# Attention's mix of a graph network: one fp32 product replaced by two rounded-fp32 products of high and low parts

## The reference

```
msg = xl[src] + xr[dst];  act = where(msg > 0, msg, 0.2 * msg)
e = sum(act * att, head)
p = exp(e - max of the node)
out[node] = sum over its edges of p * xl[src] / (sum of p + 1e-16)
```

## Time and profile before

| | us |
|---|---|
| median of 3 runs | 1897.4 |
| the profiled execution, its own time | 1914.85 |
| its span | 1913.0 |
| attention's steady part, about 468 to 889 in the span | 421 |

### The profile page before, as it was taken

One profiled execution on the slowest core, in us unless ns is written; L12 is line 12 of the kernel. 1 busy time (PEld: TensorE's weight loads), 2 busy tenths in 40 slices (PEclk: granted clock), 3 DMA queues, 4 the chain that ended last, 5 costly groups with the idle time before them and its releaser, 6 DMA issues.

```text
span 1913.0 us, 21680 instructions
## 1 busy us (share of the span) xinstructions
PE 1629.2 (85%) x8385; PEld 1359.4 (71%) x8385; DVE 844.1 (44%) x1268; ACT 454.1 (24%) x788; POOL 274.7 (14%) x265
## 2 busy tenths in 40 slices
PE   0887993745999999995549998699999989999996
PEld 0886883735777777784438887588888868878885
DVE  6785554542666755664552223432311142332233
ACT  3773111422222322221330101311201031121000
POOL 3000000015455443530220000000000000000000
PEclk9996997976878877887769999799999999999998
DMA  0345334143333332322552221422422242243221
GB/s 10 94 113 200 132 121 166 49 112 100 94 104 106 111 99 83 99 68 101 170 183 73 86 72 69 156 92 85 161 84 72 105 154 88 102 138 118 106 94 66
DMA packets 100475, 202.58 MB, mean 106 GB/s; under 512 B 24774, under 2 KB 58846, under 8 KB 100378
## 3 DMA queue, kind: packets, MB, share of 16 engines
q1 hardware_dynamic: 84474, 152.65, 23.8%
q0 software_dynamic: 15904, 48.61, 8.3%
HBM read 147.29 MB, written 53.92 MB: 105 GB/s over the span
## 4 chain that ended last, share of the span: by engine, by line
PE 42%; DMA 4%; DVE 3%; ACT 2%; DVEq 2%; issue 1%; POOL 0%; SPq 0%; POOLq 0%; ACTq 0%
PE layers_y_ps L1591 27%; PE layers_sum_ps L1555 13%; PE layers_turn_ps L1574 2%; DMA layers_raw<-in_L_gnn_W_self 1%; DMA layers_raw<-in_L_gnn_W_neigh 1%; DVE layers_w_lo L1701 1%; ACT layers_w_hi L1638 1%; DVEq L1739 1%; DMA layers_raw<-in_L_gnn_W 1%; DVE layers_y L710 1%; ACT layers_plain L1671 0%; DVEq L1745 0%; DVE layers_ln_stats L704 0%; DVEq L705 0%; DMA layers_x<-hidden_d 0%
## 5 line engine op out<-in xcount | busy, mean ns | idle before, releaser
L1138 POOL DMA_INDIRECT attention_got<-xl_d,attention_src x200 | 213.8, 1069 | 585.0 <-DMA attention_src<-in_src_held 380.7
L1744 DVE TENSOR_TENSOR layers_y<-layers_y_ps,layers_side 128x1024 f32<-128x1024 f32 x50 | 61.2, 1224 | 492.9 <-PE layers_y_ps L1591 488.6
L1591 PE MATMUL layers_y_ps<-layers_w_hi,layers_turned_hi 128*128 128x512 f32 x840 | 270.4, 404 | 9.6 <-DVE layers_turned_lo L1709 9.6
L1591 PE MATMUL layers_y_ps<-layers_w_lo,layers_turned_hi 128*128 128x512 f32 x840 | 265.6, 398 | 0.0
L1591 PE MATMUL layers_y_ps<-layers_w_hi,layers_turned_lo 128*128 128x512 f32 x840 | 263.8, 396 | 0.0
L1555 PE MATMUL layers_sum_ps<-layers_parts_hi,layers_counts 128*128 128x512 f32 x600 | 189.0, 396 | 8.7 <-POOL layers_parts_lo L1532 8.7
L1591 PEld LDWEIGHTS layers_y_ps<-layers_w_hi,layers_turned_hi 128*128 128x128 f32 x840 | 160.4, 195 | 42.7 <-DVE layers_turned_lo L1709 11.3
L1591 PEld LDWEIGHTS layers_y_ps<-layers_w_lo,layers_turned_hi 128*128 128x128 f32 x840 | 162.5, 193 | 35.1
L1555 PE MATMUL layers_sum_ps<-layers_parts_lo,layers_counts 128*128 128x512 f32 x600 | 186.3, 392 | 0.0
L1591 PEld LDWEIGHTS layers_y_ps<-layers_w_hi,layers_turned_lo 128*128 128x128 f32 x840 | 161.5, 192 | 34.9
L1555 PEld LDWEIGHTS layers_sum_ps<-layers_parts_hi,layers_counts 128*128 128x128 f32 x600 | 111.7, 190 | 31.0 <-issue 9.1
(11 more groups left out here) (247 smaller groups left out, 2231.7 us busy)
## 6 DMA issues: line engine op xcount, KB each, us to landing
layers_x<-x_d SPq DMA_DIRECT2D x40, 512.0 KB, 3.4
layers_counts<-counts_d SPq DMA_DIRECT2D x30, 640.0 KB, 3.9
attention_dst_wide<-in_dst_held SPq DMA_DIRECT2D x20, 640.0 KB
x_d<-layers_y SPq DMA_DIRECT2D x20, 512.0 KB, 2.7
self_d<-layers_y SPq DMA_DIRECT2D x20, 512.0 KB, 2.9
layers_side<-self_d SPq DMA_DIRECT2D x20, 512.0 KB, 4.2
layers_raw<-in_L_gnn_W_self POOLq DMA_DIRECT2D x16, 512.0 KB, 4.5
layers_raw<-in_L_gnn_W_neigh POOLq DMA_DIRECT2D x16, 512.0 KB, 4.3
```

What stands on the lines that cost most here:

```text
L1138: pool.indirect_dma_start(got[s][:, t, :], None, xl_d, bass.IndirectOffsetOnAxis(src[s][:, t:t + 1], 0))\
L1591: last = nc.tensor.matmul(y_ps[n % 2][:, a:a + HALF], rows_in[:, k, :], w[:, begin + k, a:a + HALF], start=(k == 0 and p == 0), stop=(k == ...
L1744: nc.vector.tensor_tensor(out, product, side[:, :], ALU.add).then_inc(y_ps_free, 1)
```

## The change

`hot` becomes a rounded-fp32 tile (F32R). The weighted rows are split: ScalarE rounds them to `mix_hi` (`take_high`), VectorE subtracts that from them and rounds the rest to `mix_lo` (`take_low`), each in two halves of 5 tiles x 260 columns. `mix` multiplies `hot` by all high tiles of the half, then by all low tiles: again 10 products per half, but rounded-fp32 ones with one record each. `take_high` of half 0 stands at the end of ScalarE's step q = 4, that of half 1 at the end of the next q = 0; `take_low` of half 0 in VectorE's q = 0 (after `find_nodes`), that of half 1 in q = 1 (after `take_best`). Both halves of `mix` come two steps later than before: half 0 in q = 1 instead of the q = 4 before it, half 1 in q = 2 instead of q = 0. `finish` moves from q = 1 to q = 2. Each loop that takes part runs one step longer.

```diff
--- before.py
+++ after.py
@@ -1059,8 +1059,10 @@
         shift = slots("shift", [P, KH, 2], F32R)
         clamped = slots("clamped", [P, SUB_TILES, HEADS])
         keep = slots("keep", [SUB, HEADS])
-        hot = slots("hot", [P, SUB_TILES, SUB])
+        hot = slots("hot", [P, SUB_TILES, SUB], F32R)
         weighted = slots("weighted", [P, SUB_TILES, HEADS, HEAD_DIM + 1])
+        mix_hi = slots("mix_hi", [P, SUB_TILES, HEADS * (HEAD_DIM + 1)], F32R)
+        mix_lo = slots("mix_lo", [P, SUB_TILES, HEADS * (HEAD_DIM + 1)], F32R)
         inverse = m.sb("inverse", [SUB, HEADS])
         mixed = slots("mixed", [SUB, HID])
         nothing = m.sb("nothing", [ROWS - SUB * SUBS, HID])
@@ -1078,7 +1080,11 @@
             m.sem(n) for n in "hot_t_ready message_ready scaled_ready bent_ready bent_r_ready scored maxed".split())
         shift_ready, shifted, clamp_ready, exp_ready, keep_ready, hot_ready = (
             m.sem(n) for n in "shift_ready shifted clamp_ready exp_ready keep_ready hot_ready".split())
-        weighed, mixed_in, out_ready = (m.sem(n) for n in "weighed mixed_in out_ready".split())
+        weighed, mix_hi_ready, mix_lo_ready, mixed_in, out_ready = (
+            m.sem(n) for n in "weighed mix_hi_ready mix_lo_ready mixed_in out_ready".split())
+
+        def half_of(tiles, half):
+            return tiles[:, half * PAIRS_HELD:(half + 1) * PAIRS_HELD]
         mixed_stored = m.sems("mixed_stored")
         block = m.block(gpsimd_works=True)
 
@@ -1202,17 +1208,19 @@
 
             def mix(j, half):
                 tiles = range(half * PAIRS_HELD, (half + 1) * PAIRS_HELD)
-                pe.wait_ge(weighed, 2 * j + half + 1)
+                pe.wait_ge(mix_lo_ready, 2 * j + half + 1)
                 if half == 0 and j >= 2:
                     pe.wait_ge(out_ready, j - 1)
-                for t in tiles:
-                    last = nc.tensor.matmul(mix_ps[j % 2][:, :, :].rearrange("p h d -> p (h d)"), hot[j % 2][:, t, :],
-                                            weighted[j % 2][:, t].rearrange("p h d -> p (h d)"), start=(t == 0),
-                                            stop=(t == SUB_TILES - 1))
+                for part in (mix_hi, mix_lo):
+                    for t in tiles:
+                        last = nc.tensor.matmul(mix_ps[j % 2][:, :, :].rearrange("p h d -> p (h d)"),
+                                                hot[j % 2][:, t, :], part[j % 2][:, t, :],
+                                                start=(t == 0 and part is mix_hi),
+                                                stop=(t == SUB_TILES - 1 and part is mix_lo))
                 if half:
                     last.then_inc(mixed_in, 1)
 
-            for i in range(LAST + PAIRS_HELD + 2):
+            for i in range(LAST + PAIRS_HELD + 3):
                 j, q = i // PAIRS_HELD, i % PAIRS_HELD
                 if i < LAST:
                     messages(i)
@@ -1220,9 +1228,9 @@
                     take_shift(j - 1)
                 if 2 <= i < LAST + 2:
                     score(i - 2)
-                if q == 4 and 1 <= j <= SUBS:
-                    mix(j - 1, 0)
-                if q == 0 and j >= 2:
+                if q == 1 and j >= 2:
+                    mix(j - 2, 0)
+                if q == 2 and j >= 2:
                     mix(j - 2, 1)
 
         @block.scalar
@@ -1258,7 +1266,13 @@
                 nc.scalar.activation(weighted[b][:, :, :, HEAD_DIM], clamped[b][:, :, :], ACT.Exp)\
                     .then_inc(exp_ready, 1)
 
-            for i in range(LAST + PAIRS_HELD):
+            def take_high(j, half):
+                act.wait_ge(weighed, 2 * j + half + 1)
+                nc.scalar.activation(half_of(mix_hi[j % 2], half).rearrange("p t c -> p (t c)"),
+                                     half_of(weighted[j % 2], half).rearrange("p t h d -> p (t h d)"), ACT.Copy)\
+                    .then_inc(mix_hi_ready, 1)
+
+            for i in range(LAST + PAIRS_HELD + 1):
                 j, q = i // PAIRS_HELD, i % PAIRS_HELD
                 if i < LAST:
                     scale(i)
@@ -1266,6 +1280,10 @@
                     exponentials(j - 1)
                 if i < LAST:
                     bend(i)
+                if q == 4 and j >= 1:
+                    take_high(j - 1, 0)
+                if q == 0 and j >= 2:
+                    take_high(j - 2, 1)
 
         @block.vector
         def _(dve):
@@ -1362,8 +1380,15 @@
                                         inverse[:, :].unsqueeze(2).to_broadcast([SUB, HEADS, HEAD_DIM]), ALU.mult)\
                     .then_inc(out_ready, 1)
 
+            def take_low(j, half):
+                dve.wait_ge(mix_hi_ready, 2 * j + half + 1)
+                nc.vector.tensor_tensor(half_of(mix_lo[j % 2], half).rearrange("p t c -> p (t c)"),
+                                        half_of(weighted[j % 2], half).rearrange("p t h d -> p (t h d)"),
+                                        half_of(mix_hi[j % 2], half).rearrange("p t c -> p (t c)").bitcast(F32),
+                                        ALU.subtract).then_inc(mix_lo_ready, 1)
+
             find_nodes(0)
-            for i in range(LAST + PAIRS_HELD + 2):
+            for i in range(LAST + PAIRS_HELD + 3):
                 j, q = i // PAIRS_HELD, i % PAIRS_HELD
                 if i < LAST:
                     bend(i)
@@ -1381,7 +1406,11 @@
                     weigh(j - 1, 0)
                 if q == 4 and 1 <= j <= SUBS:
                     weigh(j - 1, 1)
+                if q == 0 and j >= 2:
+                    take_low(j - 2, 0)
                 if q == 1 and j >= 2:
+                    take_low(j - 2, 1)
+                if q == 2 and j >= 2:
                     finish(j - 2)
 
 
```

## The result

| | us |
|---|---|
| after, median of 6 runs (1904.64 to 1912.85) | 1908.28 |
| before, median of 6 runs on the same chip (1890.76 to 1899.03) | 1896.51 |
| ratio after / before, 95% interval | 1.006 [1.0037, 1.0084] |
| after, its profiled execution | 1908.23, span 1906.4 |

The change makes the kernel slower, by a little. The forecast was 1876 us; the measured time lies inside the range, on the other side of no change.

What follows compares the result with a forecast made beforehand. TensorE was taken to bound the attention stage, at two clock prices. Mix -63, VectorE's floor +10 and clock +32 sum to -21 us: 1897.4 becomes 1876 us, with an 8-in-10 range of 1836 to 1925.

Steps and rivals of the forecast that it cites:

- the clock, +32 us: Attention stage: mix directly ahead of the shift leaves 1.5 more pairs at 1.2 GHz in 12 sub-blocks, +32 us.
- the 130 to 220: Attention stage: time at 1.2 GHz, in us, outside which the prediction's step on the clock would be wrong.
- the prediction's own price: TensorE's pairs in attention: one takes 3.84 us at half clock, 2.03 at full, so 1.81 us more.
- rival A: Attention's clock keeps its pattern or gains, so only VectorE's floor counts: -53 us, 1844 us; chance 0.22.
- the rule that the prediction cited: TensorE's clock is throttled by default and activity releases it, so a lighter mix works against the change; no size given.
- the cases that the rule leans to: Attention's clock eats the gain (1911 to 1934 us, chance 0.20), or the whole stage runs at half clock (2005 us, 0.04).
- Rival B: In attention, a half-clock first mix half no longer brings the clock back: 1911 to 1934 us, chance 0.20.
- The mix product, -63 us: TensorE's mix in attention: rounded products at 116 ns each, half clock twice that, halve its 126.5 us, saving 63.
- 60 to 70: TensorE's mix: the busy time in us to which its records should fall, from 126.5.
- VectorE's floor, +10 us: Subtractions and a wait hold full-clock attention sub-blocks near 17.1 us, not 15.4: 1.7 us lost in 6, +10 us.
- The base: Starting point: attention has 160 us at 1.2 GHz in the profiled 1914.85 us execution; -21 was taken off the 1897.4 median.

Runs made afterwards that it cites:

- run 9: The kernel before, unchanged, traced again on the second chip: median 1858.2 us, ratio 1.0013.
- run 8: The changed kernel, unchanged, timed on the second chip against the kernel before: median 1891.1 us, ratio 1.0218.
- Runs 3, 10 and 15: Kernel before with its fp32 mix moved two steps later, nothing split: ratio 0.9915 on one chip, 1.005 and 1.0041 on another.
- runs 1, 11 and 2: Kernel before with rounded products of rounded rows taken twice, no copies or subtractions: ratios 1.0063 and 1.0128 at the new place, 0.9955 at the old.
- run 12: Rounded mix at the new place without copies or subtractions, plus ten unread 252-column products per half: median 1868.4 us, 4 executions from 1837.9 to 1880.0.
- run 4: The changed kernel with its mix in fp32 from the weighted rows, copies, subtractions and waits kept: 1920.4 us, ratio to before 1.0343.
- run 13: The kernel of run 4, but TensorE waits only for the weighted rows, not the low part: 1864.9 us, ratio to before 1.006.

## Why the prediction was wrong

**The step that failed is the clock, +32 us.** I wrote "I reckon with 1.5 pairs more at half clock", in 12 of the sub-blocks, and a granted clock of 0.75 to 0.8. It was 0.66 over 412 us, which is 2 x 0.34 x 412 = 280 us at 1.2 GHz, outside the 130 to 220 that I had named as the limit. The length of a stretch was about right: from the fall at 646.4 to the first half at 657.70 lie 11.3 / 3.84 = 2.9 pairs, where before had 1.3. Their number was not: the clock falls in every sub-block. Measured by the prediction's own price, 280 - 160 = 120 us more at 1.2 GHz, of which 1.81/3.84 is lost time, make +57 us and not +32. The limits that I had named didn't follow from my sum either: 12 times 1.5 pairs of 3.84 us are 69 us more, 229 in all, a clock near 0.71. Against run 9, on one chip, the sum closes to 0.4 us: 13.63 - 3.19 = 10.4 us more at 1.2 GHz per sub-block, of which 1.81/3.84 is lost time, 4.9 us; the mix gives back 2.3, and the idle 2% of TensorE in run 9's stage another 0.4. That is +2.2 us, where 20.46 - 18.63 = 1.83 was measured. In the sub-blocks 4 to 18 it is 27.5 us, and the two traced stages differ by 27.7; the medians of run 8 and of before beside it differ by 35.7, more than these two traces explain.

**The reason behind it was wrong too.** I derived the loss from the mix's new place ahead of the shift. Runs 3, 10 and 15 have that place and 2.3 to 4.6 us at 1.2 GHz; runs 1, 11 and 2 have light products at either place and 11.7 to 13.6. What I gave as a mere remark against rival A, "TensorE's work per sub-block gets thinner by a quarter", was the cause. With the light mix the granted clock is 0.67, with the same mix filled by further products 0.84 (runs 11 and 12).
By the rule that the prediction cited from the Trainium skill ("TensorE: Matmul & The Clock Gate", section "What's actually happening"), activity releases a throttle that is otherwise there. These two runs agree with it, though TensorE's busy time doesn't tell that activity: it is 300.00 of 300 us in both. I had given the cases that the rule leans to a chance of 0.24.

**Rival B was nearest, in its result rather than in its mechanism.** The time, 1908, lies just below its lower edge of 1911. But its step, that a first half at half clock no longer brings the clock back, isn't what happened: at 659.87 the clock is back right behind each first half, as before. What changed is the fall: in before 15 of the 20 first halves ran at half clock for most of their length (the prediction counted 14, which moves its sum by 1 us), and its stretches at 1.2 GHz lasted mostly 6.8 to 10.2 us; in after it is every one, and from the fifth to the eighteenth sub-block each stretch lasts 13.6 us.

**The mix product, -63 us.** The price was right: from 641.60 to 642.79 ten take 1.19 us, 119 ns each, at full clock (116 predicted), and from 657.70 to 659.87 2.17 us at half (2.3). The product of price and number was not: busy time is 77.5 us and not 60 to 70, since all first halves run at 1.2 GHz. The gain in busy time is 49 us and not 63; what the scores alone grew by, 28 us, goes against it.

**VectorE's floor, +10 us.** Durations were right (1.50 us against 1.5, ScalarE's 1.27 against 1.3). The floor was hardly met in after, as TensorE was slower: 9.4 us of waiting, 3 times. Where TensorE's mix was long again (run 4) the wait was met, 33.5 us in 11 times from 500 to 800 us, and the sub-blocks took 21 to 25 us, partly by their time at 1.2 GHz. In run 13, which has all of VectorE's work and no such wait, the sub-blocks without time at 1.2 GHz take 16.7 to 17.6 us: so the floor by VectorE's work, 17.1 us, was not far off, and the wait was what I had too small. I had added up VectorE's work and a delay of 0.6 us; I had left out what is queued behind TensorE's waiting first half, the next messages, and so VectorE's own next input. By run 13 the work itself is nearly free and the wait is the price: a second ceiling right above the one that showed. That it works as a ring is my reading of the order; what the runs show is its price.

**The base.** 160 us at 1.2 GHz in before was one execution's, 17.5 us above the median, and I took a gain worked out on it off the median. Trace against trace the change did gain: 1914.85 to 1908.23 us, -6.6, with sub-blocks of 20.63 us instead of 21.59; the forecast for such an execution was -21. Per sub-block, 5.2 us more at 1.2 GHz cost 2.5 us, the mix gives back 2.3 and TensorE's idle time fell from 0.9 to 0.2 us; that is -0.6, where -0.96 was measured. So of the 32 us between forecast and result about 14 are errors of the sum and about 18 come from the base. The later traces of before have 3.2 to 4.6 us per sub-block, so the clock had further to fall than I reckoned with.

**What held.** The gathers, SyncE's queue and the end of the stage cost nothing visible; `dst_wide` was waited for once, 0.7 us, as in before (0.8); the projection and the layers kept their times to about 2 us.

No version beats both kernels on both chips. The fp32 mix at the new place comes nearest: 0.9915 on one, 1.004 to 1.005 on the other.

## What to carry to other kernels

Where TensorE bounds a stage and its granted clock is between the levels, don't price a lighter product by its own two durations alone: look up what activity holds the clock for the work around it, and test it by adding work as well as by taking some away. Take the clock's share from several executions, not from one. And where a new wait is put on the bounding engine, follow the ring: what is queued behind it may be what the awaited engine itself needs next.

## What the runs showed of the hardware

- An engine without any idle time can be held at 1.2 GHz for two thirds of it: 300.00 of 300 us busy at a granted clock of 0.67 (runs 8 and 11, one chip); on another chip run 1 has 299.62 of 300 and 0.67. The busy share didn't tell the clock here; with 24% more products in the same time it was 0.84 (run 12).
- A rounded-fp32 product of 260 columns and 63 weight columns starts 119 ns after the one before it at 2.4 GHz and 217 ns at 1.2 GHz; the fp32 one stands as two records 233 ns apart (641.00 to 643.33 in run 3 for ten).
- GpSimd's indirect gathers show 1216 to 1394 ns each in the kernels with the rounded copies (after 1216, run 13 1394) and 1064 to 1073 in before, for the same 200 gathers. They are long where they meet VectorE's subtractions: in after the 52 that overlap a `take_low` take 1788 ns on average, the 116 that overlap neither it nor a `weigh` 974; in run 13 it is 1853 (54) and 972 (109). Nothing waited for that here.
- The unchanged kernel before takes 1887 us on one chip and 1856 on another, and after's ratio to before is 1.006 on the chip of the result and 1.022 on the second of these: a change that turns on the granted clock should be timed on more than one chip.
